# Attention weights applied in plain 4-byte matmuls: what it does to a fused attention and linear kernel

## The chip, the cores and the metric

The kernel runs on one core of a Trainium2 chip. A core has TensorE (PE, matrix products into PSUM, with its weight loads shown apart as PEld), VectorE (DVE), ScalarE (ACT), GpSimd (POOL) and SyncE (SP, which here only issues DMAs). The metric is the device time of the whole program in microseconds (us), as a median of several runs. Each engine runs its own instruction list in order, and the lists meet at semaphores.

## What is computed

A block of a transformer on x of 4 sequences, 1024 tokens and 1024 channels: layer norm, attention with 16 heads of 64 channels, residual; then layer norm, a 1024 x 1024 linear layer, residual. Cut to what matters here:

```python
q, k, v = (split_heads(layernorm(x) @ W + b) for W, b in ((Wq, bq), (Wk, bk), (Wv, bv)))
# local: each block of 128 queries sees 256 keys around it
probs = softmax(einsum('nhbqd,nhbkd->nhbqk', q_blocks, k_windows) / 8)
ctx = einsum('nhbqk,nhbkd->nhbqd', probs, v_windows)
# global: bos, eos and the 62 tokens with the largest |q| of each head see all keys
g_probs = softmax(einsum('nhqd,nhkd->nhqk', q[idx], k) / 8)
g_ctx = einsum('nhqk,nhkd->nhqd', g_probs, v)
ctx = ctx.at[bn, bh, idx].set(g_ctx)
x = x + ctx
x = x + layernorm(x) @ (weight * scale_weight[:, None]).T + bias
```

All of it is wanted at 4-byte precision.

## The kernel before

**Number formats.** TensorE is fed mostly in `F32R`, a 4-byte format that holds fewer mantissa bits. To keep precision, an operand is split in a high part (a copy that rounds to F32R, on ACT or POOL) and a low part (the rest, a subtraction on DVE or POOL), and a product is made from several matmuls of parts. Transposes (`pe.transpose`, a matmul against the identity `ident`) take plain 4-byte `F32` operands, unsplit.

**Stages.** For each of the 4 sequences (`batch`), the transposed, normalised x (`xT_hi`, `xT_lo`) meets the q weights; then a loop runs over 8 pairs of heads. One pass of it is `attend` on PE, ACT and DVE, and `unit` on POOL: 32 units u in all. In a unit, PE works on the attention of one pair of heads, and between its steps projects keys and values of the next pair in eight parts of 12 matmuls (`part(0)` to `part(7)`, `project`, L564, 128x512 each). At the end stands a linear stage (`linear`, L751).

**Local attention of a unit** goes in 4 steps s, each with 2 blocks of queries b for the 2 heads h. `scores` (L662) fills the PSUM tile `score`; DVE takes row maxima (`maxima`), ACT the exponentials with row sums (`exps`, L988) into `probs`; PE transposes these in `turn_p` (L677) into the PSUM tile `turn`. ACT copies `turn` to `pT_hi` (`p_hi_out`, L1001), DVE subtracts to get `pT_lo` (`p_lo_out`, L1380). `weigh` (L687) multiplies by V: for each of the 4 (head, block) groups g, 4 matmuls, `pT_hi` and `pT_lo` as the stationary operand for 2 tiles of keys c, against `v_nat`, which holds the 64 channels of V's high part and the 64 of its low part side by side. So one matmul is 128x128 and g takes 128 columns of the PSUM tile `pv`: sums with V's high part in the first 64, with its low part in the last 64.

**Out of `pv`.** ACT copies the low half (`pv_lo_out`, L1012), DVE adds the high half (`pv_sums`, L1401) into `pv_sum` and frees `pv` for the next step (`pv_free`), and POOL multiplies by the reciprocals of the row sums (`normalise`, L449) into `ctx_out`, one of two buffers by the parity of s. SP stores it to DRAM (`store_ctx`, L255).

**Global attention of a unit** does the same once for all 1024 keys: `turn_gp` (L722), `gp_hi_out`, `gp_lo_out`, then `global_weigh` (L731) with 2 times 9 matmuls of 128x256 (both heads, high and low), `g_lo_out` and `g_out` into `g_ctx`.

**V** comes from `vT` by `turn_v` (L699) into the PSUM tile `misc`, from which `v_hi_out` (ACT) and `v_lo_out` (DVE) make `v_nat`.

**What sets the order** is the program as written: `attend` on each engine is a fixed list, given below. On PE a unit ends with `part(6)`, `part(7)`, `global_weigh`, and the next begins with `scores(0)`.

## Time and profile before

| | us |
|---|---|
| median of 3 runs | 2184.9 (2182.88 to 2185.11) |
| profiled execution | 2185.36 |
| its span | 2183.8 |
| PE busy | 2142.9 (98%) |
| PEld busy | 1825.5 (84%) |
| DVE busy | 1475.5 (68%) |
| ACT busy | 836.9 (38%) |
| POOL busy | 600.7 (28%) |

The span goes from the first to the last instruction of the profiled execution. A busy share says how long an engine had something in hand, not how fast: a matmul's shown duration reaches from its start to a modelled end, and matmuls overlap, so what one costs PE is read from the distance between starts, or from the chain of waits. The granted clock of TensorE is 9 (90% or more of full speed) in every one of 40 slices.

### The profile page before, as it was taken

The page shows a single profiled execution, that of the slowest core. Times are in us where ns is not written, and L with a number is a line of the kernel's source. Part 1 is how long each engine was busy: PE and PEld are TensorE (multiplying, and loading weights), DVE is VectorE, ACT ScalarE, POOL GpSimd, SP SyncE. Part 2 cuts the span into 40 slices and gives each one's busy share as a digit, 9 for nine tenths or more (in the row PEclk, how much of TensorE's full clock was granted, in tenths as well). Part 3 has the DMA queues.
Part 4 walks back from the last instruction along what each step waited for, and adds up shares of the span by engine and source line. Part 5 has one row for each costly group of instructions (what it writes and reads, how often), then busy time and mean ns, then how long its engine had stood idle before and what let it go on. Part 6 is the DMA issues. An engine that isn't in the chain of part 4 may idle for free.

```text
span 2183.8 us, 38335 instructions
## 1 busy us (share of the span) xinstructions
PE 2142.9 (98%) x12768; PEld 1825.5 (84%) x12768; DVE 1475.5 (68%) x2966; ACT 836.9 (38%) x2203; POOL 600.7 (28%) x464
## 2 busy tenths in 40 slices
PE   6999999999999999999999999999999998999999
PEld 5888888888888888888888888888888887888887
DVE  5687667665876776648776767496666675666664
ACT  3334444453344455523444545325445451000000
POOL 2332232224321332243223312433123113121221
PEclk9999999999999999999999999999999999999999
DMA  4332121104322211043122211321113113333331
GB/s 148 96 97 73 60 89 44 53 30 125 99 64 70 74 58 52 30 125 97 63 72 60 71 53 32 99 83 45 53 51 108 34 49 121 132 132 134 127 141 68
DMA packets 116725, 175.38 MB, mean 80 GB/s; under 512 B 16208, under 2 KB 81814, under 8 KB 116624
## 3 DMA queue, kind: packets, MB, share of 16 engines
q1 hardware_dynamic: 108976, 156.30, 22.3%
q10 hardware_dynamic: 4320, 15.73, 1.8%
q0 software_dynamic: 3328, 2.17, 0.5%
q8 instruction: 43, 0.70, 0.1%
q14 instruction: 58, 0.48, 0.1%
HBM read 122.73 MB, written 51.44 MB: 80 GB/s over the span
## 4 chain that ended last, share of the span: by engine, by line
PE 88%; DVE 5%; issue 3%; ACT 2%; POOL 1%; DMA 1%; DVEq 0%; SPq 0%; POOLq 0%; ACTq 0%
PE proj L564 44%; PE proj L751 15%; PE pv L687 9%; PE turn L677 5%; PE score L662 5%; PE pv L731 3%; PE score L712 2%; PE misc L699 1%; PE turn L740 1%; PE turn L722 1%; DVE xT_lo L1276 1%; PE turn L605 1%; ACT probs L988 1%; ACT xT_hi L916 1%; DMA q_store<-in_rows 0%
## 5 line engine op out<-in xcount | busy, mean ns | idle before, releaser
L564 PE MATMUL proj<-xT_hi,w_hi 128*128 128x512 f32 x1568 | 410.0, 403 | 9.7 <-DVE xT_lo L1268 3.8
L564 PE MATMUL proj<-xT_hi,w_lo 128*128 128x512 f32 x1568 | 416.9, 397 | 0.0
L564 PE MATMUL proj<-xT_lo,w_hi 128*128 128x512 f32 x1568 | 389.1, 390 | 0.0
L564 PEld LDWEIGHTS proj<-xT_lo,w_hi 128*128 128x128 f32 x1568 | 294.3, 188 | 63.4
L564 PEld LDWEIGHTS proj<-xT_hi,w_lo 128*128 128x128 f32 x1568 | 287.0, 188 | 63.5
L564 PEld LDWEIGHTS proj<-xT_hi,w_hi 128*128 128x128 f32 x1568 | 281.6, 189 | 66.3 <-issue 5.4
L988 ACT ACTIVATE probs<-score,neg_max 128x256 f32<-128x256 f32 (+1 forms) x512 | 229.2, 460 | 162.3 <-DVE neg_max L1364 98.7
L449 POOL TENSOR_TENSOR ctx_out<-pv_sum,row_inv 128x256 f32<-128x256 f32 x128 | 84.9, 663 | 661.4 <-DVE pv_sum L1401 635.4
L425 POOL CAST w_hi<-w_raw 128x1024 fp32r<-128x1024 f32 x96 | 115.5, 1203 | 515.1 <-PE proj L564 357.8
L427 POOL TENSOR_TENSOR w_lo<-w_raw,w_hi 128x1024 fp32r<-128x1024 f32 x96 | 232.0, 2416 | 7.8
L687 PE MATMUL pv<-v_nat,pT_lo 128*128 128x128 f32 x1024 | 198.1, 275 | 0.0
L687 PE MATMUL pv<-v_nat,pT_hi 128*128 128x128 f32 x1024 | 194.3, 271 | 0.0
L1380 DVE TENSOR_TENSOR pT_lo<-turn,pT_hi 128x512 fp32r<-128x512 f32 x256 | 164.6, 684 | 13.9 <-ACT pT_hi L1001 10.8
L687 PEld LDWEIGHTS pv<-v_nat,pT_hi 128*128 128x128 f32 x1024 | 162.1, 191 | 11.4 <-issue 0.8
L1401 DVE TENSOR_TENSOR pv_sum<-pv,pv_lo 128x256 f32<-128x256 f32 x128 | 54.3, 424 | 153.1 <-ACT pv_lo L1012 138.9
L687 PEld LDWEIGHTS pv<-v_nat,pT_lo 128*128 128x128 f32 x1024 | 155.4, 192 | 0.0
L544 POOL TENSOR_TENSOR q_store<-q_store,bias_b 128x1024 f32<-128x1024 f32 x30 | 71.6, 2389 | 261.2 <-DVE q_store L1631 259.9
L968 ACT ACTIVATE kT_hi<-proj,bk_c 128x512 fp32r<-128x512 f32 x64 | 44.2, 690 | 255.3 <-PE proj L564 159.0
L1001 ACT CAST pT_hi<-turn 128x512 fp32r<-128x512 f32 x256 | 138.7, 594 | 7.6 <-PE turn L677 2.1
L677 PE MATMUL turn<-ident,probs 128*128 128x128 f32 (+1 forms) x1024 | 135.6, 275 | 2.0 <-ACT probs L988 2.0
L1282 DVE TENSOR_TENSOR q_sq<-q_nat 128x512 f32<-128x512 f32 x64 | 69.3, 1083 | 93.9 <-ACT q_nat L938 80.3
L677 PEld LDWEIGHTS turn<-ident,probs 128*128 128x128 f32 (+1 forms) x1024 | 111.8, 137 | 4.2 <-ACT probs L988 3.7
(173 smaller groups left out, 3409.7 us busy)
## 6 DMA issues: line engine op xcount, KB each, us to landing
w_raw<-in_wstream SPq DMA_DIRECT2D x96, 512.0 KB
x_buf<-in_rows SPq DMA_DIRECT2D x55, 512.0 KB, 3.9
q_rows<-q_nat SPq DMA_DIRECT2D x64, 256.0 KB
ctx_rows<-ctx_out SPq DMA_DIRECT2D x128, 128.0 KB, 1.8
q_store<-ctx_rows SPq DMA_DIRECT2D x30, 512.0 KB
out<-q_store ACTq DMA_DIRECT2D x30, 512.0 KB, 2.6
q_store<-in_cols SPq DMA_DIRECT2D x28, 512.0 KB, 4.0
q_store<-in_rows SPq DMA_DIRECT2D x8, 512.0 KB, 5.4
```

What stands on the lines that cost most here:

```text
L425: pool.tensor_copy(w_hi[b][:, :], w_raw[b][:, :]).then_inc(w_hi_set, 1)
L427: pool.tensor_tensor(w_lo[b][:, :], w_raw[b][:, :], w_hi[b][:, :].bitcast(F32), ALU.subtract).then_inc(w_split[b], 1)
L449: pool.tensor_tensor(ctx_out[:, s % 2].rearrange("p b h d -> p h b d"), pv_sum[:, s % 2].rearrange("p (h b) d -> p h b d", h=2), row_inv[: ...
L544: pool.tensor_tensor(lin_hb[:, b, :], lin_h[:, b, :], bias_b[:, :], ALU.add).then_inc(hb_set, 1)
L564: mm = pe.matmul(proj[:, bank, :], w[b][:, k * P:k * P + P], x[:, k, half * HALF:half * HALF + HALF], start=(m == 0), stop=(m == 23), skip ...
L662: mm = pe.matmul(score[:, at:at + hi - lo], qs[r, i * BLK:i * BLK + BLK], ks[r, lo:hi], start=(first and b == 0), stop=stop, skip_group_ch ...
L677: mm = pe.transpose(turn[0:rows, col:col + P], probs[:, src:src + rows], ident[:, :])
L687: mm = pe.matmul(pv[:, g * P:g * P + P], pt[:, (g * 2 + c) * P:(g * 2 + c) * P + P], v_nat[:, 2 * s + b + c, h, :], start=(m == 0), stop=( ...
L751: mm = pe.matmul(proj[:, half, :], x[b][:, k * P:k * P + P], w[:, k, half * 512:half * 512 + 512], start=(m == 0), stop=(m == 23), skip_gr ...
L988: last = act.activation(probs[:, at:at + hi - lo], score[:, at:at + hi - lo], ACT.Exp, bias=neg_max[:, g:g + 1], accum_out=row_sum[:, g:g ...
L1001: act.copy(pT_hi[:, h * 512:h * 512 + 512], turn[:, h * 512:h * 512 + 512]).then_inc(pT_hi_set, 1)
L1380: dve.tensor_tensor(pT_lo[:, cols], turn[:, cols], pT_hi[:, cols].bitcast(F32), ALU.subtract).then_inc(pT_set, 1)
```

## The change

The probabilities are copied out of `turn` once, as plain 4-byte `pT` (ACT, `p_out`, `gp_out`), and V out of `misc` once, as plain 4-byte `v_nat` with 64 columns per head (ACT, `v_nat_out`). `weigh` multiplies them in 8 matmuls of 128x64 per step instead of 16 of 128x128, `global_weigh` in 9 of 128x128 instead of 18 of 128x256. `pv` then holds the full sums, and DVE multiplies them by the reciprocals straight into `ctx_out` (`pv_out`), or into `g_ctx` (`g_out`). POOL's `normalise` is gone, with the subtractions on DVE and the copies of low halves on ACT. The wait for the store of `ctx_out` two steps earlier moves from POOL to DVE.

```diff
-        v_nat = sb("v_nat", [P, TILES + 1, 2, P], F32R)
+        v_nat = sb("v_nat", [P, TILES + 1, 2, HD])
-        pT_hi, pT_lo = sb("pT_hi", [P, SEQ + P], F32R), sb("pT_lo", [P, SEQ + P], F32R)
+        pT = sb("pT", [P, SEQ + P])
...
             def store_ctx(n, hp, s):
-                sp.wait_ge(ctx_set, n * (PAIRS * STEPS) + hp * STEPS + s + 1 + STEPS)
+                sp.wait_ge(pv_free, n * (PAIRS * EVENTS) + hp * EVENTS + s + 2)
...
-                for s in range(STEPS - 1):
-                    normalise(n, hp, s)
                 if value:
                     split_value(n, hp)
-                normalise(n, hp, STEPS - 1)
...
                     for b in range(2):
                         g = h * 2 + b
-                        for m, (pt, c) in enumerate(((pT_hi, 0), (pT_hi, 1), (pT_lo, 0), (pT_lo, 1))):
-                            mm = pe.matmul(pv[:, g * P:g * P + P], pt[:, (g * 2 + c) * P:(g * 2 + c) * P + P],
-                                           v_nat[:, 2 * s + b + c, h, :], start=(m == 0), stop=(m == 3))
+                        for c in range(2):
+                            mm = pe.matmul(pv[:, g * HD:g * HD + HD], pT[:, (g * 2 + c) * P:(g * 2 + c) * P + P],
+                                           v_nat[:, 2 * s + b + c, h, :], start=(c == 0), stop=(c == 1))
...
-                for m, pt in enumerate((pT_hi, pT_lo)):
-                    for j in range(TILES + 1):
-                        col = ((j - 1) % (TILES + 1)) * P
-                        mm = pe.matmul(pv[:, 0:256], pt[:, col:col + P], v_nat[:, j, :, :].rearrange("p h d -> p (h d)"),
-                                       start=(m == 0 and j == 0), stop=(m == 1 and j == TILES))
+                for j in range(TILES + 1):
+                    col = ((j - 1) % (TILES + 1)) * P
+                    mm = pe.matmul(pv[:, 0:P], pT[:, col:col + P], v_nat[:, j, :, :].rearrange("p h d -> p (h d)"),
+                                   start=(j == 0), stop=(j == TILES))
...
-            def p_hi_out(u, s):
+            def p_out(u, s):
                 for h in range(2):
                     act.wait_ge(p_turned, 2 * (u * EVENTS + s) + h + 1)
-                    act.copy(pT_hi[:, h * 512:h * 512 + 512], turn[:, h * 512:h * 512 + 512]).then_inc(pT_hi_set, 1)
+                    act.copy(pT[:, h * 512:h * 512 + 512], turn[:, h * 512:h * 512 + 512]).then_inc(pT_set, 1)
...
-            def pv_sums(u, s):
-                dve.wait_ge(pv_lo_set, u * EVENTS + s + 1)
-                dve.wait_ge(ctx_set, u * STEPS + s + STEPS - 1)
-                dve.tensor_tensor(pv_sum[:, s % 2], pv4[:, :, 0:HD], pv_lo[:, :, :], ALU.add).then_inc(pv_free, 1)
+            def pv_out(u, s):
+                dve.wait_ge(pv_done, u * EVENTS + s + 1)
+                dve.wait_ge(inv_set, u * EVENTS + s + 1)
+                dve.wait_ge(ctx_stored[s % 2], u * (16 * STEPS // 2) + 16 * (s // 2) + 16)
+                dve.tensor_tensor(ctx_out[:, s % 2].rearrange("p b h d -> p h b d"),
+                                  pv[:, 0:4 * HD].rearrange("p (h b d) -> p h b d", h=2, b=2),
+                                  row_inv[:, 4 * s:4 * s + 4].rearrange("p (h b) -> p h b", h=2).unsqueeze(3)
+                                  .broadcast_to([P, 2, 2, HD]), ALU.mult).then_inc(pv_free, 1)
...
-                dve.wait_ge(pv_lo_set, u * EVENTS + EVENTS)
-                dve.tensor_tensor(g_sum[0:64, :], pv4[0:64, 0, 0:HD], pv_lo[0:64, 0, :], ALU.add)
-                dve.tensor_tensor(g_sum[64:P, :], pv4[64:P, 1, 0:HD], pv_lo[64:P, 0, :], ALU.add).then_inc(pv_free, 1)
-                dve.wait_ge(pv_free, u * EVENTS + EVENTS + 1)
-                dve.tensor_scalar(g_ctx[:, bass.ds(hp, 1), :].rearrange("p a d -> p (a d)"), g_sum[:, :],
-                                  row_inv[:, 4 * STEPS:4 * STEPS + 1], None, ALU.mult).then_inc(g_set, 1)
+                dve.wait_ge(pv_done, u * EVENTS + EVENTS)
+                dve.wait_ge(inv_set, u * EVENTS + EVENTS)
+                for h in range(2):
+                    r = slice(h * HD, h * HD + HD)
+                    last = dve.tensor_scalar(g_ctx[r, bass.ds(hp, 1), :].rearrange("p a d -> p (a d)"),
+                                             pv[r, h * HD:h * HD + HD], row_inv[r, 4 * STEPS:4 * STEPS + 1], None, ALU.mult)
+                last.then_inc(pv_free, 1)
```

On PE, in a unit, the weighing of step 1 stands between the projection's matmuls and the transposes of step 2. Before:

```order
L564 MATMUL proj<-xT_hi,w_hi 128x512 x8
L564 MATMUL proj<-xT_hi,w_lo 128x512 x4
L681 REGISTER_ALU
L687 MATMUL pv<-v_nat,pT_hi 128x128 x2
L687 MATMUL pv<-v_nat,pT_lo 128x128 x2
L687 MATMUL pv<-v_nat,pT_hi 128x128 x2
L687 MATMUL pv<-v_nat,pT_lo 128x128 x2
L687 MATMUL pv<-v_nat,pT_hi 128x128 x2
L687 MATMUL pv<-v_nat,pT_lo 128x128 x2
L687 MATMUL pv<-v_nat,pT_hi 128x128 x2
L687 MATMUL pv<-v_nat,pT_lo 128x128 x2
L668 ISA
```

And the same place now (line numbers are those of the changed program):

```order
L544 MATMUL proj<-xT_hi,w_hi 128x512 x8
L544 MATMUL proj<-xT_hi,w_lo 128x512 x4
L661 REGISTER_ALU
L667 MATMUL pv<-v_nat,pT 128x64 x8
L648 ISA
L657 MATMUL turn<-ident,probs 128x128 x4
```

Sixteen matmuls are eight of half the width; their place has not moved.

On DVE, the stretch of a unit from the maxima of step 1 to those of step 2 (`neg_max` are the maxima, `row_inv` the reciprocals of the row sums, `top_idx` belongs to the search for the global tokens). Before:

```order
L1364 TENSOR_REDUCE neg_max<-score 128x2 x2
L1390 REGISTER_ALU
L1394 RECIPROCAL row_inv<-row_sum 128x4
L1317 MAX_INDEX top_idx<-top_val,x_norm 8x8
L1305 REGISTER_ALU
L1346 REGISTER_ALU
L1349 TENSOR_TENSOR v_nat<-misc,v_nat 128x2x64
L1401 TENSOR_TENSOR pv_sum<-pv,pv_lo 128x256
L1379 REGISTER_ALU
L1380 TENSOR_TENSOR pT_lo<-turn,pT_hi 128x512
L1379 REGISTER_ALU
L1380 TENSOR_TENSOR pT_lo<-turn,pT_hi 128x512
```

And now:

```order
L1318 TENSOR_REDUCE neg_max<-score 128x2 x2
L1331 REGISTER_ALU
L1333 RECIPROCAL row_inv<-row_sum 128x4
L1280 MAX_INDEX top_idx<-top_val,x_norm 8x8
L1268 REGISTER_ALU
L1338 ISA
L1339 TENSOR_TENSOR ctx_out<-pv,row_inv 128x2x2x64
L1313 REGISTER_ALU
L1318 TENSOR_REDUCE neg_max<-score 128x2 x2
```

The three subtractions for V and the probabilities are gone, the addition has become the multiplication that POOL did, and the maxima of the next step stand right behind it.

## Rows read from the trace of the kernel before

**Rows 1.** the page: busy us of each engine (share of span), granted clock

```profile
PE 2142.9 (98%) x12768; PEld 1825.5 (84%) x12768; DVE 1475.5 (68%) x2966; ACT 836.9 (38%) x2203; POOL 600.7 (28%) x464
...
PEclk9999999999999999999999999999999999999999
```

**Rows 2.** waits of PE, whole span: total us, times, longest

```profile
PE score L599 <- DVE q_store L1223: 15.2, 1, 15.2
PE proj L751 <- DVE qT_lo L1471: 4.3, 1, 4.3
...
PE turn L677 <- ACT probs L988: 2.0, 9, 0.3
PE turn L740 <- issue: 1.9, 1, 1.9
PE pv L731 <- DVE pT_lo L1386: 1.5, 1, 1.5
```

**Rows 3.** chain of waits, 826 to 846 us: start, us, what

```profile
833.08 1.74 PE pv L687 x16
...
838.62 5.46 PE proj L564 x24
```

**Rows 4.** timeline of PE, end of a unit: start us, us, group

```profile
837.59 1.04 PE L722 MATMUL turn<-ident,probs 128*128 128x128 f32 x8
838.38 2.07 PE L564 MATMUL proj<-xT_hi,w_hi 128*128 128x512 f32 x8
...
842.10 1.98 PE L564 MATMUL proj<-xT_lo,w_hi 128*128 128x512 f32 x8
843.92 1.24 PE L731 MATMUL pv<-v_nat,pT_hi 128*128 128x256 f32 x9
844.99 1.24 PE L731 MATMUL pv<-v_nat,pT_lo 128*128 128x256 f32 x9
846.16 0.50 PE L662 MATMUL score<-kT_hi,qT_hi 64*128 64x192 f32 x4
```

**Rows 5.** weight loads by shape: busy us, mean ns of one

```profile
L687 PEld LDWEIGHTS pv<-v_nat,pT_lo 128*128 128x128 f32 x1024 | 155.4, 192 | 0.0
...
L722 PEld LDWEIGHTS turn<-ident,probs 128*128 128x128 f32 x224 | 25.4, 140 | 3.8
...
L615 PEld LDWEIGHTS score<-ident,norms 128*8 128x8 f32 x64 | 5.5, 87 | 1.9
...
L722 PEld LDWEIGHTS turn<-ident,probs 128*64 128x64 f32 x32 | 3.6, 111 | 0.0
```

**Rows 6.** groups of PE by shape, same columns

```profile
L564 PE MATMUL proj<-xT_lo,w_hi 128*128 128x512 f32 x1568 | 389.1, 390 | 0.0
...
L731 PE MATMUL pv<-v_nat,pT_lo 128*128 128x256 f32 x288 | 39.7, 283 | 0.0
```

**Rows 7.** groups of DVE by shape, same columns

```profile
L1380 DVE TENSOR_TENSOR pT_lo<-turn,pT_hi 128x512 fp32r<-128x512 f32 x256 | 164.6, 684 | 13.9 <-ACT pT_hi L1001 10.8 <-issue 0.2
...
L1401 DVE TENSOR_TENSOR pv_sum<-pv,pv_lo 128x256 f32<-128x256 f32 x128 | 54.3, 424 | 153.1 <-ACT pv_lo L1012 138.9 <-issue 13.6
```

**Rows 8.** the group on POOL that goes, from the page

```profile
L449 POOL TENSOR_TENSOR ctx_out<-pv_sum,row_inv 128x256 f32<-128x256 f32 x128 | 84.9, 663 | 661.4 <-DVE pv_sum L1401 635.4
```

**Rows 9.** the copy on ACT that goes, by shape

```profile
L1012 ACT COPY pv_lo<-pv 128x256 f32<-128x256 f32 x128 | 47.6, 372 | 109.7 <-PE pv L687 109.7
```

**Rows 10.** timeline of ACT, one local step: the four Exp of step 1 end

```profile
812.94 0.48 ACT L988 ACTIVATE probs<-score,neg_max 128x256 f32<-128x256 f32 x1
813.29 0.21 ACT L988 ACTIVATION_READ_ACCUMULATOR probs<-score,neg_max 128x1 f32 x1
```

**Rows 11.** timeline of PE behind them: the transposes that need those Exp

```profile
814.83 1.06 PE L677 MATMUL turn<-ident,probs 128*128 128x128 f32 x8
```

**Rows 12.** the tile ctx_rows: its stores, and DMA time to landing

```profile
L255 SPq DMA_DIRECT2D ctx_rows<-ctx_out x128: 372/373/539, 166.0 to 1809.8; - x128
...
DMA to landing us min/median/max: 1.8/1.8/9.4
```

More of the change, by code:

```diff
@@ L969, in k_hi_out, with v_nat_out @@
                                bias=bk_c[:, bass.ds(hp, 1)]).then_inc(k_hi_set[h], 1)
-            def v_hi_out(u, g):
+            def v_nat_out(u, g):
                 act.wait_ge(m_turned, u * MISC + g + 1)
                 for rows, j, step, count, col in V_PIECES[g]:
-                    last = act.copy(v_nat[0:rows, j:j + step * (count - 1) + 1:step, :, 0:HD],
+                    last = act.copy(v_nat[0:rows, j:j + step * (count - 1) + 1:step, :, :],
                                     misc[0:rows, col:col + count * P].rearrange("p (t h d) -> p t h d", h=2, d=HD))
-                last.then_inc(m_hi_set, 1)
+                last.then_inc(m_set, 1)
             def gq_hi_out(u):
@@ L1046, in attend @@
                     ahead_hi(0)
-                v_hi_out(u, 0)
+                v_nat_out(u, 0)
                 exps(u, 0)
@@ L1051, in attend @@
                     ahead_hi(1)
-                v_hi_out(u, 1)
-                p_hi_out(u, 0)
+                v_nat_out(u, 1)
+                p_out(u, 0)
                 exps(u, 1)
@@ L1056, in attend @@
                 columns(1)
-                v_hi_out(u, 2)
-                pv_lo_out(u, 0)
-                p_hi_out(u, 1)
+                v_nat_out(u, 2)
+                p_out(u, 1)
                 exps(u, 2)
                 columns(2)
-                pv_lo_out(u, 1)
-                p_hi_out(u, 2)
+                p_out(u, 2)
                 exps(u, 3)
@@ L1066, in attend @@
                     out(1, 0)
-                pv_lo_out(u, 2)
                 gq_hi_out(u)
-                p_hi_out(u, 3)
+                p_out(u, 3)
                 columns(4)
@@ L1343, in top_rows @@
                     dve.wait_ge(base_set, n + 2)
-            def v_lo_out(u, g):
-                dve.wait_ge(m_hi_set, u * MISC + g + 1)
-                for rows, j, step, count, col in V_PIECES[g]:
-                    tiles = slice(j, j + step * (count - 1) + 1, step)
-                    last = dve.tensor_tensor(v_nat[0:rows, tiles, :, HD:P],
-                                             misc[0:rows, col:col + count * P].rearrange("p (t h d) -> p t h d", h=2, d=HD),
-                                             v_nat[0:rows, tiles, :, 0:HD].bitcast(F32), ALU.subtract)
-                last.then_inc(m_set, 1)
             def gq_lo_out(u):
-                dve.wait_ge(m_hi_set, u * MISC + MISC)
+                dve.wait_ge(m_hi_set, u + 1)
                 dve.tensor_tensor(gq_lo[:, :], misc[:, 0:P], gq_hi[:, :].bitcast(F32), ALU.subtract).then_inc(m_set, 1)
@@ L1374, in global_maxima @@
                                   negate=True).then_inc(max_set, 2)
-            def p_lo_out(u, s):
-                for h in range(2):
-                    cols = slice(h * 512, h * 512 + 512)
-                    dve.wait_ge(pT_hi_set, 2 * (u * EVENTS + s) + h + 1)
-                    dve.tensor_tensor(pT_lo[:, cols], turn[:, cols], pT_hi[:, cols].bitcast(F32),
-                                      ALU.subtract).then_inc(pT_set, 1)
-            def gp_lo_out(u):
-                dve.wait_ge(pT_hi_set, 2 * (u * EVENTS + EVENTS))
-                dve.tensor_tensor(pT_lo[:, 0:1024], turn[:, :], pT_hi[:, 0:1024].bitcast(F32), ALU.subtract)
-                dve.tensor_tensor(pT_lo[:, 1024:1152], misc[:, 0:P], pT_hi[:, 1024:1152].bitcast(F32),
-                                  ALU.subtract).then_inc(pT_set, 2)
             def inverses(u, s):
                 dve.wait_ge(exp_set, 2 * (u * EVENTS + s + 1))
-                if s < STEPS:
-                    dve.wait_ge(ctx_set, u * STEPS + s + 1)
                 size = 4 if s < STEPS else 1
                 dve.reciprocal(row_inv[:, 4 * s:4 * s + size], row_sum[:, 4 * s:4 * s + size]).then_inc(inv_set, 1)
-            pv4 = pv[:, :].rearrange("p (g d) -> p g d", g=4)
-            def pv_sums(u, s):
-                dve.wait_ge(pv_lo_set, u * EVENTS + s + 1)
-                dve.wait_ge(ctx_set, u * STEPS + s + STEPS - 1)
-                dve.tensor_tensor(pv_sum[:, s % 2], pv4[:, :, 0:HD], pv_lo[:, :, :], ALU.add).then_inc(pv_free, 1)
+            def pv_out(u, s):
[6 more added lines that the diff above has]
+                                  .broadcast_to([P, 2, 2, HD]), ALU.mult).then_inc(pv_free, 1)
             def pad_q(n, u, hp, half):
@@ L1505, in attend @@
                 columns(1)
-                v_lo_out(u, 2)
-                pv_sums(u, 0)
-                p_lo_out(u, 1)
+                pv_out(u, 0)
                 maxima(u, 2)
@@ L1512, in attend @@
                 columns(2)
-                pv_sums(u, 1)
-                p_lo_out(u, 2)
+                pv_out(u, 1)
                 if ahead:
@@ L1525, in attend @@
                     lin_moments(0, 0, 0)
-                pv_sums(u, 2)
+                pv_out(u, 2)
                 gq_lo_out(u)
-                p_lo_out(u, 3)
                 if ahead:
@@ L1540, in attend @@
                     k_lo_out(n, hp + 1, 0)
-                pv_sums(u, 3)
+                pv_out(u, 3)
                 if not last:
```

47 lines of the change are left out of this document (9 added, 38 removed).

## The prediction

> **What bounds the kernel now.** I read the page first, then PE's waits, then one steady unit in the chain and the timeline. PE is busy 2142.9 of 2183.8 us at the full clock [rows 1]; 15.2 us of the rest is the start, and the four other waits that this change could touch are 9.7 us together [rows 2]. In the steady unit the chain never leaves PE: weighing follows projection follows weighing [rows 3]. DVE, ACT and POOL wait for PE, not the reverse. So a microsecond taken from them is worth nothing, and one added to PE's own list is paid 32 or 128 times. The whole question is what PE pays for a weighing.
>
> **What a weighing costs now.** The 16 matmuls of a local step hold the chain for 1.74 us, 0.109 us each [rows 3]. The 18 of the global one take 846.16 - 843.92 = 2.24 us, 0.124 each [rows 4]. Over 32 units: 128 x 1.74 = 223 us and 32 x 2.24 = 72 us.
>
> **What such a pair of weight load and matmul is made of.** A matmul of 512 columns shows 390 ns, one of 256 columns 283 [rows 6]: 107/256 = 0.42 ns a column, the 2.4 GHz level, so 27, 53 and 107 ns for 64, 128 and 256 columns. A weight load of a plain 4-byte operand shows 87, 111 and 140 ns for 8, 64 and 128 columns: 84 ns that don't hold up the next, and 56 ns of loading for 128 columns. A load of an F32R part shows 192, so 108 ns of loading [rows 5]. Now compare with what a pair costs from start to start:
> - F32R, 128 columns: load 108, stream 53, and 109 measured [rows 3]. That is the longer of the two: the load runs under the stream of the matmul before. For 256 columns 108 and 107, measured 124; for 512, 108 and 214, measured (843.92 - 842.10)/8 = 227 [rows 4]. The same.
> - Plain 4-byte (the transposes): load 56, stream 53, and (838.38 - 837.59)/8 = 99 measured [rows 4]. That is near the sum, 109, and far from the longer, 56. Here the load doesn't seem to run under the stream.
>
> **The change on PE.** A local step becomes 8 matmuls of 64 columns, the global one 9 of 128, all with plain 4-byte operands. The trace of before has plain operands only in transposes, which move values and don't multiply them at full precision, so a true product isn't shown and must be bounded. The products kept so far are four (high and low by high and low), and the new matmul must make the same four. I take it as two passes, one for each part of the stationary operand, each with a load of its own and with both parts of the moving operand streamed: 2 x 64 = 128 columns in a local pass, 2 x 128 = 256 in a global one. That is exactly the work of the present matmuls, in pairs: 16 passes a step, 18 for the global one. What differs is whether the loads hide.
>
> I take the load at 108 ns (a load of a part, as the present ones are) and, as in the only rows with plain operands, in line with the stream:
> - local: (108 + 53) x 16 = 2.58 us against 1.74, +0.84, x 128 = +107 us;
> - global: (108 + 107) x 18 = 3.87 us against 2.24, +1.63, x 32 = +52 us.
>
> Bounds of this term. Below: one load and one short stream per matmul, at the price of one transpose pair, 0.099: 0.79 and 0.89 us, so -122 and -43 = -165 us. Above: four passes, each with a load of 108 in line with its 64 or 128 columns: 4 x 135 x 8 = 4.32 us and 4 x 161 x 9 = 5.80 us, +330 and +114 = +444 us. Both ends are far; I stay with the two serial passes because they stand on measured pieces. Four passes with the cheaper load of 56 come to the same by another way: 4 x 83 x 8 = 2.66 and 4 x 109 x 9 = 3.92 us, +118 and +54 = +172.
>
> The rule that bears on the number of passes speaks against the change. The Trainium skill (FP8 and Floating Point Precision, TensorE Precision Notes) has a true 4-byte product go through the array four times, high by high, high by low, low by high, low by low; it doesn't say how often weights are loaded, and no row here shows it. The sum by it is anything from the fastest rival below to the slowest.
>
> **The change on the other engines, all of it beside PE's work.**
> - DVE loses the subtractions for probabilities, 256 x 684 ns = 165 us busy and more for the global ones and V; the addition of 424 ns becomes a multiplication of the same shape from the same PSUM tile, at about the same price [rows 7]. ACT loses 128 copies of 372 ns [rows 9], POOL 128 multiplications, 85 us [rows 8]. All are at 68, 38 and 28% busy [rows 1] and were waiting: value nothing, save for the waits of PE that they end. Those are 1.5 us for `pT_lo` before the global weighing, and parts of the 1.9 and 4.3 us at the start of the linear stage [rows 2]. I take -3 us; at most it is their sum and the 2.0 on `probs`, -10, and at least 0.
> - `pT` is ready on ACT's copy, without the subtraction behind it, and `pv` is free after one DVE instruction instead of ACT and DVE. Both come earlier than they are needed already.
> - DVE takes over the wait for the store of `ctx_out` two steps before. Behind it in DVE's list stand the maxima of the next step, for which ACT's Exp and then PE's transposes wait. A store lands in 1.8 us, 9.4 at worst [rows 12], and between two steps lie, twice, a weighing of 1.74 us [rows 3] and 12 projection matmuls of 0.227 [rows 4], 8.9 us without the rest; I take 0. If it failed once in a unit by 1 us, it would be 32 us.
> - SP's stores now wait for DVE rather than POOL, one instruction earlier. Nothing.
>
> **Sum.** Against the profiled execution: 2185.4 + 107 + 52 - 3 = 2341 us. The median of the runs is 0.5 us lower, which changes nothing.
>
> **The rivals.**
> 1. *The loads hide after all (not slower).* Plain passes then cost what F32R ones of equal columns do: 16 x 0.109 = 1.74 and 18 x 0.124 = 2.24 us, a difference of 0, and 2182 with the waits. For it: the work per pass is the same, and the present loads hide. Against it: the transposes' 99 ns. Its place is every weighing, and what decides is whether a load in the midst of two passes may run under the stream; if a local pass stays under 110 ns, the change is not slower.
> 2. *Serial, but with the transposes' load of 56.* Local 16 x 109 = 1.74 us, no change; global 18 x 163 = 2.93, +0.69 x 32 = +22: 2204.
> 3. *One load, four streams (faster).* A local matmul is then an F32R one of 256 columns, 0.124: 0.99 us, -0.75 x 128 = -96; a global one is one of 512, 0.227: 2.05 us, -0.19 x 32 = -6: 2080 with the waits. Against it: a part is loaded for each product that has another stationary part, and there are two. PE would then come earlier to the transposes behind: the Exp of that step end at 813.50 and PE wants them at 814.83 [rows 10, 11], so 0.75 us can be taken from the step before ACT is waited for.
> 4. *Four whole pairs per matmul.* At the transposes' 99 ns, whatever the columns: 4 x 99 x 8 = 3.17 us, +1.43 x 128 = +183, and 4 x 99 x 9 = 3.56, +1.32 x 32 = +42: 2407. At 109 ns a pair, 3.49 and 3.92 us: +224 and +54, 2460. For it: the transposes are the plain matmuls that the trace has, and they needn't form products of parts. The Trainium skill (TensorE: Matmul & The Clock Gate, Terms) calls transpose mode four times faster for 4-byte operands, which by itself would put an ordinary plain matmul at four such pairs and the time at this rival's 2407; nothing in the trace shows it.
>
> **How the numbers follow.** Forecast (serial passes, 2341, or 2353 by the cheap-load variant) 0.42; rival 1 0.24; rival 2 0.08; rival 3 0.13; rival 4 0.13. About 0.2% (4.4 us) is what can be told from no change. Slower by more: forecast, rivals 2 and 4 and a hundredth of rival 1, 0.64. Faster by more: rival 3 and a third of rival 1, in which the ended waits bring more than 3 us, 0.21. The rest, 0.15, is the same. The likeliest case by itself spans 2310 to 2370. The range goes from 2172, which takes in rival 1 with all waits gained, to 2430, which takes in the nearer form of rival 4; outside stay rival 3 and the dearer rival 4, 0.18.
>
> **What would show it.** In the profile after, the chain's piece for 8 local matmuls at 2.6 us and for the 9 global ones at 3.9, with PE still at 98% and no new waits, each unit longer by 4 x 0.84 + 1.63 = 5.0 us; loads of `pT` at about 192 ns, twice as many in the records as there are matmuls in the program. Pieces of 1.74 and 2.24 us would mean rival 1, about 1 us rival 3, over 3 us rival 4. Wrong in another way would be waits of PE on `probs` or `pv`, or DVE waiting at `ctx_out` for a DMA. A total near 2341 with other pieces would be luck, not the theory.

## The result, and the profile after

| | before | after |
|---|---|---|
| median of 4 runs each on one chip, us | 2184.5 (2182.9 to 2185.1) | 2165.3 (2164.1 to 2165.5) |
| ratio, 95% interval | | 0.991 (0.990 to 0.993) |
| span of the profiled execution, us | 2183.8 | 2163.8 |
| VectorE, ScalarE, GpSimd busy | 68, 38, 28% | 56, 36, 24% |

The change takes 19.3 us off, 0.9%. The forecast was 2341; the range ended at 2172, above the result. PE's granted clock is at the full level (2.4 GHz) in both kernels, but for a stretch near the start and one at the start of the linear stage; the second is not equally long in the two profiles, and is taken up below.

The page: PE's busy time falls by 11.9 us from that of [rows 1], its share and its number of recorded matmuls don't move.

```profile
PE 2131.0 (98%) x12768; PEld 1819.7 (84%) x12768; DVE 1206.7 (56%) x2486; ACT 783.3 (36%) x2011; POOL 509.1 (24%) x336
```

The local weighing, as one line's instructions: duration min/median/max, first and last start.

```profile
L667 PEld LDWEIGHTS pv<-v_nat,pT x2048: 187/192/245, 160.3 to 1786.8; 128*128 128x128 f32 x187
L667 PE MATMUL pv<-v_nat,pT x2048: 217/275/275, 160.4 to 1786.9; 128*128 128x64 f32 x187
```

The program has 128 steps of 8 such matmuls, 1024; the records hold 2048, each with a weight load of 192 ns like those of [rows 5]. So a plain 4-byte product is two passes with a load each.

The chain of waits in a steady unit (start, us, what), to be read against [rows 3]: 16 passes still hold it for 1.73 us.

```profile
820.75 1.73 PE pv L667 x16
```

The timeline of PE at the same unit's end, against [rows 4]: the global weighing goes from 838.45 to 840.55, 2.10 us, where it was 2.24.

```profile
838.45 2.17 PE L710 MATMUL pv<-v_nat,pT 128*128 128x128 f32 x18
840.55 0.50 PE L642 MATMUL score<-kT_hi,qT_hi 64*128 64x192 f32 x4
```

PE's waits, against [rows 2]: the one for `pT_lo` is gone, that for `probs` has fallen from 2.0 to 0.3 us, and `qT_lo` is as long as before.

```profile
PE proj L730 <- DVE qT_lo L1413: 4.3, 1, 4.3
...
PE turn L719 <- DVE x_norm L1186: 1.4, 1, 1.4
...
PE turn L657 <- ACT probs L967: 0.3, 1, 0.3
```

These waits explain some 4 us, the global weighing 32 x 0.14 = 4.5. To find the rest I measured every unit on PE's timeline, from the end of one global weighing to the end of the next (the end is taken as the start of the matmul behind it). The fourth sequence has no next one to prepare, so its last units stand apart:

| us | ordinary unit | 7th unit, sequences 1 to 3 | 8th unit, sequences 1 to 3 | last two, sequence 4 | from the last unit to PE's last matmul |
|---|---|---|---|---|---|
| before | 42.45 | 42.67 | 45.28 | 44.16, 48.63 | 362.15 |
| after | 42.26 | 42.26 | 42.17 | 42.17, 46.59 | 360.79 |

20 ordinary units give 3.8 us, three 7th ones 1.2, three 8th ones 9.3, the last two of sequence 4 give 2.0 each and the end 1.4; with 0.2 at the start, 19.9 of the 20.0 us between the spans. Nearly half of the gain lies in three units of 32, which the steady unit of the prediction doesn't show.

The 1.4 us at the end are the clock's, not the change's, but for a tenth. At the start of the linear stage the granted clock lies at the lower level (1.2 GHz) for 6.8 us in the profile of before and for 3.4 us in that of after (the line of before, then that of after; window, us, PE busy, granted clock, DMA share, GB/s):

```profile
1834.60:1841.40 6.80, 5.29 (x13) 0.50 0.40 150
...
1817.50:1820.90 3.40, 3.40 (x10) 0.50 0.40 116
```

Experiment 3 below is the kernel after with matmuls added only behind this stage. Its profile has 6.8 us at the lower level here, and 362.06 us from the last unit to the last projection where after has 360.79. So this term changes from one execution to the next under one and the same program.

Here is the 8th unit of the first sequence before, on PE (start, us, group, idle before and its releaser):

```profile
449.67 0.50 PE L662 MATMUL score<-kT_hi,qT_hi 64*128 64x192 f32 x4
...
452.38 2.08 PE L564 MATMUL proj<-xT_hi,w_hi 128*128 128x512 f32 x8 [1.20 <-DVE xT_lo L1276]
...
455.58 0.63 PE L699 MATMUL misc<-ident,vT 128*128 128x128 f32 x4 [0.19 <-DVE v_nat L1349]
...
469.69 0.66 PE L677 MATMUL turn<-ident,probs 128*128 128x128 f32 x4 [0.19 <-ACT probs L988]
470.60 0.66 PE L677 MATMUL turn<-ident,probs 128*128 128x128 f32 x4 [0.26 <-ACT probs L988]
```

And the same unit after:

```profile
448.14 0.50 PE L642 MATMUL score<-kT_hi,qT_hi 64*128 64x192 f32 x4
...
449.41 2.07 PE L544 MATMUL proj<-xT_hi,w_hi 128*128 128x512 f32 x8
...
465.72 1.04 PE L657 MATMUL turn<-ident,probs 128*128 128x128 f32 x8
```

From the unit's start the projection begins 452.38 - 449.67 = 2.71 us in before, 1.27 after: 1.44 us. The transposes at 469.69 begin 20.02 in, those at 465.72 after 17.58: by then it is 2.44, and the unit ends 3.11 apart. The four waits marked here sum to 1.84 us, less than is lost: a wait counts only while the engine has nothing in hand, and the stretches that merely thin out carry none. Compare starts, not only waits.

What DVE does ahead of that projection, before:

```profile
441.60 4.33 DVE L1276 TENSOR_TENSOR xT_lo<-q_store,xT_hi 128x512 fp32r<-128x512 f32 x2
445.86 1.21 DVE L1385 TENSOR_TENSOR pT_lo<-turn,pT_hi 128x1024 fp32r<-128x1024 f32 x1
...
447.85 4.29 DVE L1276 TENSOR_TENSOR xT_lo<-q_store,xT_hi 128x512 fp32r<-128x512 f32 x2
```

And POOL beside it, splitting the next projection weights:

```profile
441.09 1.50 POOL L425 CAST w_hi<-w_raw 128x1024 fp32r<-128x1024 f32 x1 [8.16 <-PE proj L564]
442.67 2.72 POOL L427 TENSOR_TENSOR w_lo<-w_raw,w_hi 128x1024 fp32r<-128x1024 f32 x1
...
447.53 1.30 POOL L425 CAST w_hi<-w_raw 128x1024 fp32r<-128x1024 f32 x1 [1.11 <-issue]
448.91 2.69 POOL L427 TENSOR_TENSOR w_lo<-w_raw,w_hi 128x1024 fp32r<-128x1024 f32 x1
```

Each pair of subtractions for the next sequence's columns, which have both inputs in SBUF, takes 4.3 us. Taken one by one, the first of a pair takes 1.5 us beside POOL's cast and the second 2.9 beside POOL's subtraction; the second of the first pair reads so:

```profile
443.06 2.88 DVE L1276 TENSOR_TENSOR xT_lo<-q_store,xT_hi 128x512 fp32r<-128x512 f32 x1
```

After, both subtractions of the first pair begin before POOL's cast does, at 439.92, and both stay at 0.68 to 0.69 us. One collision is left, spread over the next two subtractions, 1.46 and 2.88 us:

```profile
439.31 1.29 DVE L1239 TENSOR_TENSOR xT_lo<-q_store,xT_hi 128x512 fp32r<-128x512 f32 x2
...
440.58 1.46 DVE L1239 TENSOR_TENSOR xT_lo<-x_buf,xT_hi 128x512 fp32r<-128x512 f32 x1
441.96 3.48 DVE L1239 TENSOR_TENSOR xT_lo<-q_store,xT_hi 128x512 fp32r<-128x512 f32 x2
```

Alone a pair takes 1.29 us; beside POOL up to 4.33. This is what the experiments had to test, beside the price of the passes.

### The profile page after: what moved, and what is told of

Its sections match the earlier page's. It is cut to its first block, busy times and chain, and to the rows that moved or that the text cites. A ratio compares the mean times of both kernels' runs of the same rounds, so it can differ in the third digit from the quotient of the medians.

```text
span 2163.8 us, 36898 instructions
## 1 busy us (share of the span) xinstructions
PE 2131.0 (98%) x12768; PEld 1819.7 (84%) x12768; DVE 1206.7 (56%) x2486; ACT 783.3 (36%) x2011; POOL 509.1 (24%) x336
## 4 chain that ended last, share of the span: by engine, by line
PE 94%; DVE 3%; issue 1%; POOL 1%; DMA 1%; ACT 0%; SPq 0%; DVEq 0%; POOLq 0%; ACTq 0%
PE proj L544 48%; PE proj L730 15%; PE pv L667 10%; PE score L642 5%; PE turn L657 5%; PE pv L710 3%; PE score L692 2%; PE misc L679 2%; PE turn L702 1%; PE turn L719 1%; PE turn L585 1%; DMA q_store<-in_rows 1%; DVE top_idx L1280 0%; DVE x_norm L1282 0%; DVE top_val L1278 0%
## 5 line engine op out<-in xcount | busy, mean ns | idle before, releaser
L420 POOL CAST w_hi<-w_raw 128x1024 fp32r<-128x1024 f32 x96 | 106.1, 1105 | 1184.0 <-PE proj L544 912.9
L667 PEld LDWEIGHTS pv<-v_nat,pT 128*128 128x128 f32 x2048 | 246.0, 192 | 10.8
L667 PE MATMUL pv<-v_nat,pT 128*128 128x64 f32 x2048 | 242.2, 271 | 0.0
L980 ACT COPY pT<-turn 128x512 f32<-128x512 f32 x256 | 137.9, 593 | 119.4 <-PE turn L657 119.4
L1318 DVE TENSOR_REDUCE neg_max<-score 128x2 f32<-128x512 f32 x128 | 82.5, 686 | 145.9 <-PE score L642 145.9
L1339 DVE TENSOR_TENSOR ctx_out<-pv,row_inv 128x256 f32<-128x256 f32 x128 | 54.1, 423 | 165.4 <-PE pv L667 142.1
L1263 DVE SCALAR_TENSOR_TENSOR kT_lo<-proj,bk_c,kT_hi 128x512 fp32r<-128x512 f32 x64 | 47.8, 747 | 147.3 <-ACT kT_hi L947 147.2
L1321 DVE TENSOR_REDUCE neg_max<-score 128x1 f32<-128x192 f32 (+1 forms) x256 | 82.2, 384 | 49.1 <-PE score L642 49.1
L967 ACT ACTIVATION_READ_ACCUMULATOR probs<-score,neg_max 128x1 f32 x512 | 104.3, 204 | 0.0
```

Source lines behind the costliest of these rows:

```text
L420: pool.tensor_copy(w_hi[b][:, :], w_raw[b][:, :]).then_inc(w_hi_set, 1)
L667: mm = pe.matmul(pv[:, g * HD:g * HD + HD], pT[:, (g * 2 + c) * P:(g * 2 + c) * P + P], v_nat[:, 2 * s + b + c, h, :], start=(c == 0), sto ...
L967: last = act.activation(probs[:, at:at + hi - lo], score[:, at:at + hi - lo], ACT.Exp, bias=neg_max[:, g:g + 1], accum_out=row_sum[:, g:g ...
L980: act.copy(pT[:, h * 512:h * 512 + 512], turn[:, h * 512:h * 512 + 512]).then_inc(pT_set, 1)
L1318: last = dve.tensor_reduce(neg_max[:, g:g + 2], score4[:, 2 * h:2 * h + 2, a:z], AX.X, ALU.max, negate=True)
L1321: last = dve.tensor_reduce(neg_max[:, g + b:g + b + 1], score4[:, 2 * h + b, a:z], AX.X, ALU.max, negate=True)
```

## The experiments

All ratios are against the kernel before, run on the same chip.

**1. Only PE's matmuls changed.** The kernel before with plain products in its two weighings; DVE, ACT and POOL keep all their instructions.

```diff
-                        for m, (pt, c) in enumerate(((pT_hi, 0), (pT_hi, 1), (pT_lo, 0), (pT_lo, 1))):
-                            mm = pe.matmul(pv[:, g * P:g * P + P], pt[:, ...],
+                        for c in range(2):
+                            mm = pe.matmul(pv[:, g * P:g * P + HD], pT_hi[:, ...],
...
-                act.copy(pv_lo[:, :, :], pv4[:, :, HD:P]).then_inc(pv_lo_set, 1)
+                act.mul(pv_lo[:, :, :], pv4[:, :, 0:HD], 0.0).then_inc(pv_lo_set, 1)
```

> The kernel before with only TensorE's weighing changed: 8 plain 4-byte matmuls of 64 columns a step, 9 of 128 in the global one. ACT, DVE and POOL keep every instruction (the subtractions give zeros, and the low half of pv is the high one times zero). Theory (the plain matmul is two passes at the F32R price, and most of the 19 us came from DVE's relief in the last unit of each sequence): only the 0.19 us a unit from the global weighing, 32 x 0.19 = 6 us, so 2178 us, and the last unit of a sequence still takes 45.3 us. Rival (the gain is all in the matmuls): 2165 us.

Measured: 2179.9 against 2185.0, ratio 0.998 (0.997 to 0.999), -5.0 us. A steady unit falls from 42.45 to 42.26, exactly as after; the 8th stays at 45.24. Its chain:

```profile
822.37 1.73 PE pv L687 x16
```

So the plain products alone cost nothing and bring a quarter of the gain, nearly all of it in the global weighing.

**2. Only the relief.** The kernel after, with the F32R matmuls back and the low parts as constant zeros, so that DVE, ACT and POOL have the changed work and PE the old.

```diff
-                        for c in range(2):
-                            mm = pe.matmul(pv[:, g * HD:g * HD + HD], pT[:, ...],
+                        for m, (pt, c) in enumerate(((pT, 0), (pT, 1), (pZ, 0), (pZ, 1))):
+                            mm = pe.matmul(pv[:, g * P:g * P + P], pt[:, ...],
```

> The changed kernel with TensorE's F32R matmuls of before put back (16 of 128 columns a step, 18 of 256): ACT, DVE and POOL do what the changed kernel has them do. The low parts are left out: they are tiles of zeros, so the context is computed from high parts alone. Theory: the waits of PE in the last unit of each sequence go as in the changed kernel (about 13 us), the 6 us in the matmuls don't: 2171 us, last units of 42.4 us. Rival (all in the matmuls): 2184 us.

Measured: 2171.5, ratio 0.994 (0.992 to 0.996), -13.5 us. Steady units 42.45, 8th ones 42.37. The parts nearly add up: 5.0 + 13.5 = 18.5 of 19.3. Some 70% of the gain is work taken from engines that PE was said not to wait for.

**3. The price of each kind of matmul.** The kernel after, with 12 blocks of 48 matmuls or transposes behind the last projection.

```diff
+            block(48, lambda i: pe.transpose(turn[:, 0:P], probs[:, ...], ident[:, :]))
+            block(48, lambda i: pe.transpose(turn[0:64, 0:P], probs[:, ...], ident[:, :]))
+            block(48, lambda i: pe.matmul(sc[:, 0:64], pT[:, ...], vT[:, 0:64], ...))
...
+            block(48, lambda i: pe.matmul(sc[:, 0:16], xT_hi[:, ...], xT_lo[:, 0, 0:16], ...))
```

> The changed kernel with twelve blocks of 48 matmuls on TensorE behind its last matmul, whose results nobody reads: the price of each kind by itself. Theory (each plain product is two passes of load and stream, loads of 108 ns under the streams): 0.22 us a matmul with 16, 32 or 64 moving columns, 0.23 with 128, 0.45 with 256; F32R 0.109 with 16 or 128. With 64 stationary columns half the load: 0.11 to 0.13 for 64 moving ones. Rival (the load stands in line, as I predicted): 0.32 us for 64 moving columns, 0.24 for 16, 0.43 for 128. The transposes at 0.099: if their load stands in line, 64 stationary columns bring them to about 0.07; if something in the stream of 128 columns sets them, they stay at 0.099.

One run, 2281.6 us with the blocks. The timeline of PE over the blocks (in a group, 64*... or 128*... is the stationary operand's rows and columns, then the output):

```profile
2160.26 5.41 PE L875 MATMUL turn<-ident,probs 128*128 128x128 f32 x48
2165.50 5.40 PE L876 MATMUL turn<-ident,probs 128*64 128x128 f32 x48
2170.74 10.83 PE L877 MATMUL score<-vT,pT 128*128 128x64 f32 x96
2181.41 18.06 PE L878 MATMUL score<-vT,pT 128*128 128x16 f32 x96
...
2212.66 20.89 PE L880 MATMUL score<-vT,pT 128*128 128x256 f32 x96
2233.47 5.81 PE L881 MATMUL score<-vT,pT 128*64 128x64 f32 x96
2239.12 7.79 PE L882 MATMUL score<-vT,pT 128*64 128x16 f32 x96
2246.84 10.50 PE L883 MATMUL score<-xT_lo,xT_hi 128*128 128x128 f32 x48
2257.15 10.35 PE L884 MATMUL score<-xT_lo,xT_hi 128*128 128x16 f32 x48
2267.35 5.36 PE L885 MATMUL score<-xT_lo,xT_hi 128*64 128x128 f32 x48
```

And the stretches of it (window, us, PE busy, granted clock, DMA share, GB/s):

```profile
2160.30:2165.40 5.10, 5.10 (x49) 1.00 0.25 103
2165.60:2170.60 5.00, 5.00 (x48) 1.00 0.01 3
2170.80:2181.40 10.60, 10.60 (x97) 1.00 0.00 0
2181.50:2199.30 17.80, 17.80 (x97) 0.58 0.00 1
2199.30:2212.60 13.30, 13.30 (x97) 0.80 0.01 1
2212.70:2233.40 20.70, 20.70 (x98) 1.00 0.00 1
...
2239.20:2246.80 7.60, 7.60 (x98) 0.70 0.01 2
2246.90:2257.10 10.20, 10.20 (x49) 0.50 0.00 0
2257.20:2267.30 10.10, 10.10 (x49) 0.50 0.01 2
```

From start to start, a plain pass of 64 columns costs (2181.41 - 2170.74)/96 = 0.111 us, one of 256 columns 0.217, and one of 64 columns with half the stationary operand 0.059. So with 128 stationary columns the load sets the price up to where the stream is longer, and never is it the sum, 0.161 and 0.323. The blocks with a clock between the levels, plain passes of 16 and of 128 moving columns, give no price. (A plain pass streams each column twice: 2 x 64 x 0.42 = 54 ns, and 2 x 256 x 0.42 = 215, as measured.) F32R passes at the 1.2 GHz level cost 0.215 with 128 moving columns and 0.213 with 16, and 0.108 with half the stationary operand: load-bound as well. The Trainium skill (TensorE: Matmul & The Clock Gate, LDWEIGHTS (loading the stationary operand)) gives a load in ns as its column count divided by 1.2, which makes an estimate of 107 ns for 128 columns. The passes of 128 stationary columns at the full level agree, 0.108 us in the chain and 0.111 here; those at the 1.2 GHz level take twice that.

The first two rows break the inference behind the forecast. The transposes cost 0.109 us with 128 stationary columns and 0.109 with 64, both at the full level. A load in line with the stream would have made the second cheaper by half a load, 28 ns. What does hold a transpose at 0.109 is left open: fewer moving columns were not tried.

**4. The normalisation back on POOL.** The kernel after, in which DVE copies `pv` out, POOL multiplies and sets off the store.

```diff
-                dve.tensor_tensor(ctx_out[:, s % 2]..., pv[:, 0:4 * HD]..., row_inv[...], ALU.mult).then_inc(pv_free, 1)
+                dve.tensor_copy(pv_sum[:, s % 2]..., pv[:, 0:4 * HD]).then_inc(pv_free, 1)
...
+                pool.tensor_tensor(ctx_out[:, s % 2]..., pv_sum[:, s % 2]..., row_inv[...], ALU.mult).then_inc(ctx_set, 1)
```

> The changed kernel with the normalisation back on POOL: DVE copies pv to SBUF (same size as its multiplication), POOL multiplies by the reciprocals, as before. Theory (moving the normalisation is worth nothing, since DVE's list is as long and POOL is idle most of the time): 2165 us. Rival (part of the gain came from taking POOL's 85 us and its handshake with DVE away): 2170 us or more, with waits of DVE on ctx_out.

Measured: 2164.7, 0.991 (0.989 to 0.993): the same as after. Moving the multiplication is worth nothing here.

**5 to 7. Which property of the subtractions counts?** All on the kernel after. Number 5 puts subtractions of the old shapes back on DVE, on constants, for nobody; number 6 puts a one-column DVE instruction into the chain from ACT to PE instead, so that PE waits for DVE again but DVE is as light as after; number 7 has number 5's load in the last two units of each sequence only.

```diff
+                waste_v(hp, 0)
...
+                waste_v(hp, 1)
+                waste_p(hp, 0)
...
+                dve.wait_ge(pT_hi_set, 2 * (u * EVENTS + s) + h + 1)
+                dve.tensor_copy(junk[:, 3 + 2 * s + h:4 + 2 * s + h], ident[:, 0:1]).then_inc(pT_set, 1)
...
+                if isinstance(hp, int) and hp >= PAIRS - 2:
```

> The changed kernel with subtractions of the sizes removed put back into DVE's list at their old places, on constants in SBUF; nobody waits for them and they wait for nobody. Theory A (the waits in the last units come from DVE's list being too long there): most of the 13.5 us of relief is lost, 2176 to 2179 us. Theory B (they come from the subtraction standing in the chain from ACT's copy to the next matmul): 2165 us.

> The changed kernel with DVE put back into the chain only: after each of ACT's copies of V and of the probabilities, DVE waits for it, does an instruction of one column, and only that lets PE go on. Theory A (length of DVE's list): 2165 to 2168 us. Theory B (the chain): 2176 us or more.

> As the run with all the unwaited subtractions, but only in the last two of the eight units of a sequence. Theory A (only those units are short of DVE, for they also carry the low parts of the next sequence's x): the same time as with all of them. Rival (the other six units lose a little each too): nearer to 2165 us by a quarter of the difference or more.

Measured: 2168.9 (0.992, 0.991 to 0.994), 2164.7 (0.991, 0.989 to 0.992) and 2167.5 (0.992, 0.990 to 0.994). The extra link costs nothing, so it isn't latency. The dummy load costs 2.7 us against the runs of before on its own chip, 3.6 against after, far less than the 11 us or more of theory A, and not where I looked for it: the 8th units stay at 42.17, and it is the 7th unit of sequence 4 that grows from 42.17 to 46.69 (43.70 in number 7). The load alone doesn't give the 3.1 us per 8th unit.

Nor is that one unit the price of the real subtractions. The dummies read two SBUF operands, the real ones read one of theirs from PSUM, and at 1712.32 us two dummies take 4.54 us beside POOL's additions of the bias. PE then waits 0.85 and 0.26 us for `probs`, in number 7 as in number 5. Behind these waits the granted clock of number 5 falls:

```profile
1725.60:1729.20 3.60, 3.60 (x10) 0.50 0.00 0
```

In number 7 it stays at 1.00 over the same stretch. The 3.0 us between the two numbers here are the clock's.

**8. A stream twice as wide.** The kernel after, with 128 moving columns in the local product, of which half the result is thrown away; DVE reads the other half in two instructions.

```diff
-                            mm = pe.matmul(pv[:, g * HD:g * HD + HD], pT[:, ...], v_nat[:, 2 * s + b + c, h, :],
+                            mm = pe.matmul(pv[:, g * P:g * P + P], pT[:, ...], v_nat[:, 2 * s + b + c, :, :]...,
```

> The changed kernel with twice the moving columns in each local product: both heads' V (128 columns) though only 64 of the results are read; the output is complete, and DVE reads them in two instructions instead of one. Theory (the stream runs over the next load of 108 ns and is paid only above it): a pass goes from 0.108 to 0.117 us, as in the global weighing, 128 x 16 x 0.009 = +18 us, 2183. Rival (load and stream in line, as I predicted): 53 ns more a pass, +109 us, 2274.

Measured: 2170.2, 0.993 (0.992 to 0.995), 4.9 us over after, or 4.0 if each is taken against the runs of before on its own chip: over 2048 passes, 2.0 to 2.4 ns each. In line, 54 ns more stream in each of them would be 109 us. The chain:

```profile
821.81 1.78 PE pv L667 x16
```

0.111 us a pass instead of 0.108. The stream of 107 ns still lies under the load of 108. My expectation of 0.117 a pass and 2183 us, taken from the global weighing, was too high: those 18 passes are 0.117 on average up to the start of the next group, but 0.112 from one to the next inside the group.

**9 to 11. What makes the 8th unit late.** All on the kernel after: number 9 has the real subtractions, which PE waits for; number 10 lets DVE's dummy subtractions wait for ACT while PE doesn't wait for them; number 11 has the old way out of `pv` (ACT copies, DVE adds, POOL multiplies) and no subtractions.

```diff
+                    dve.tensor_tensor(pT_lo[:, cols], turn[:, cols], pT[:, cols], ALU.subtract).then_inc(pT_set, 1)
...
+                    dve.wait_ge(pT_set, 2 * (u * EVENTS + s) + h + 1)
+                    waste(P, 512, s % 2 * 1024 + h * 512)
...
+                act.mul(pv_lo[:, :, :]..., pv[:, 0:4 * HD], 0.0).then_inc(pv_lo_set, 1)
```

> The changed kernel with DVE's subtractions back as they were, reading PSUM behind ACT's copies and with PE waiting for them; the way out of pv stays the new one. Theory C (neither length nor link alone, but the two together: DVE is held by ACT, then works 1.4 us or more, and the low parts of the next x slip into POOL's weight splits): most of the 13.5 us relief is lost, 2174 to 2178 us, last units of 45 us. Rival (it was the way out of pv, with its four engines): 2165 us.

> As the run with unwaited subtractions of constants, but each waits for ACT's copy as the real ones did; PE waits for none of them. If what matters is DVE held back in its own list (waiting for ACT, then working): near the run with the real subtractions, 2174 us or more. If PE's own wait for them matters: 2169 us, as without the waits.

> The changed kernel with the old way out of pv (ACT copies, here times zero; DVE adds; POOL multiplies), and no subtractions. Theory C: 2165 to 2168 us, last units of 42.2 us. Rival (the way out of pv): 2174 us or more.

Measured: 2166.6 (0.992, 0.990 to 0.993), 2169.3 (0.993, 0.991 to 0.995) and 2166.5 (0.992, 0.990 to 0.994). The 8th units: 42.39, 42.40 and 42.20. Number 9 was expected at 2174 us or more and misses by over 7. Neither half of the old work makes them late; both together, which is number 1, give 45.24. The reason stands in DVE's rows at this place. With the real subtractions (number 9) both pairs of column subtractions miss POOL's split:

```profile
438.87 1.29 DVE L1240 TENSOR_TENSOR xT_lo<-q_store,xT_hi 128x512 fp32r<-128x512 f32 x2
...
444.03 1.28 DVE L1240 TENSOR_TENSOR xT_lo<-q_store,xT_hi 128x512 fp32r<-128x512 f32 x2
```

With the old way out (number 11) the first is caught, the second not:

```profile
439.31 4.33 DVE L1271 TENSOR_TENSOR xT_lo<-q_store,xT_hi 128x512 fp32r<-128x512 f32 x2
...
444.58 1.28 DVE L1271 TENSOR_TENSOR xT_lo<-q_store,xT_hi 128x512 fp32r<-128x512 f32 x2
```

Before, both are, and in number 1 too. One collision of 3.0 us fits into DVE's slack ahead of the next projection, two don't. In sequence 4 the last two units go to 43.01 and 47.68 in number 9, and stay at 42.16 and 46.57 in number 11: there, the subtractions cost time without the old way out.

**12. The collision removed.** The kernel before, in which POOL splits only the first column of each key and value weight inside the units (the projections use stale weights; POOL's instructions and signals stay).

```diff
-                pool.tensor_copy(w_hi[b][:, :], w_raw[b][:, :]).then_inc(w_hi_set, 1)
+                pool.tensor_copy(w_hi[b][:, 0:w], w_raw[b][:, 0:w]).then_inc(w_hi_set, 1)
...
+                split(n, i, 0, n * BUFS + PAIRS // 2 + 2 + hp, 0, n * SLICES + i, w=1)
```

> The kernel before with POOL's splits of the key and value weights inside the units cut to one column: the weights used there are stale, so keys and values are not the right ones. Theory D (in the last units DVE's SBUF to SBUF subtractions for xT_lo take 2.1 us instead of 0.65 while POOL splits weights, and this is what makes DVE late): the last units of a sequence fall from 45.3 to 43 us or less, and the time to 2176 us or less. Rival (DVE's list is too long with or without it): 45 us and 2183 us or more.

Measured: 2176.4 against 2184.3, 0.996 (0.995 to 0.998), -7.9 us, with everything that the change removes still in place. The 8th units fall from 45.28 to 42.80, 3 x 2.5 = 7.4 us, and the 7th ones from 42.67 to 42.45, 0.7 in all; sequence 4 (44.16, 48.73) doesn't move. DVE's two pairs, at the place of those 4.33 and 4.29 us:

```profile
439.59 1.28 DVE L1276 TENSOR_TENSOR xT_lo<-q_store,xT_hi 128x512 fp32r<-128x512 f32 x2
...
443.14 1.29 DVE L1276 TENSOR_TENSOR xT_lo<-q_store,xT_hi 128x512 fp32r<-128x512 f32 x2
```

That is the collision shown: the same instructions of DVE, in the same order, lose 3 us a pair only while POOL reads and writes whole weights. POOL's list is shorter here too, which could have helped by itself if DVE had waited for POOL. It didn't: in before, DVE has no idle time at this place from 439.40 to 455.43 us. The Trainium skill (SBUF — State Buffer, SBUF: two separate sides) has the rule: a DVE operation with two SBUF inputs and a GpSimd operation that reads SBUF take one pair of ports, exclusively and for a whole instruction, and the later one blocks. The rows agree: each subtraction of the pair ends 0.54 to 0.55 us behind the POOL instruction that it met (443.13 against 442.59, 445.94 against 445.39), little less than the 0.68 it takes alone.

Sequence 4 has a collision of its own, which this experiment leaves in place. In its 7th unit before, two `xT_lo` subtractions, at 1759.74 and 1762.55, take 2.9 us each beside POOL's additions of the bias, `pT_lo` is made behind them, and PE waits 1.54 us for it. In after nothing of POOL's stands at that place. What the last two units gain, 2.0 us each, is in part this collision and in part the subtractions themselves (0.8 and 1.1 in number 9, where nothing collides there); no run separates the two.

No kernel beat the one after by more than the runs differ.

## Why the prediction was wrong

Two steps failed. The first, the load in line, put the forecast 159 us too high. With it mended the sum comes to some 2177 us, and what is left, the 12 us down to 2165 and past the end of the range at 2172, is in the main the second: the relief of the other engines.

- **PE bounds the kernel, and only its own list counts.** True of a steady unit, and false of the whole. The chain and timeline of [rows 3, 4] are one ordinary unit; in the 8th unit of a sequence DVE also makes the next sequence's columns, and PE waits for it. "Worth nothing" was read from one stretch and applied to 32.
- **Two passes, each with its own load, each streaming both parts.** Right: twice as many records, loads of 192 ns as foreseen, and in experiment 3 a price of 0.217 for 256 moving columns, which is two streams of each.
- **The load in line with the stream.** This is the first step that failed, and by far the larger: 2.58 and 3.87 us were predicted for a local and a global weighing, 1.73 and 2.10 measured, so +107 and +52 us became about -1 and -4.5. The inference was that the transposes' 99 ns (109 in the block of 48) is the sum of 56 and 53. Experiment 3 shows it isn't: half the load leaves it at 109. Two numbers that happen to sum to a third had been taken for a mechanism, against the F32R rows that showed the opposite for the same engine. Experiment 8 shows the hiding from the other side.
- **Rival 1** had it: a local pass under 110 ns, and no slower. It was given 0.24. Its time, 2182, missed what the other engines give, and the 4.5 us of the global weighing: a global pass is a little cheaper than an F32R one of the same stream, 2.10/18 = 0.117 against 0.124, which neither had.
- **The relief of the other engines, -3 us.** The second step that failed, mis-sized: 13.5 (experiment 2). The waits named there did end, `pT_lo` 1.5 us, `probs` 1.7, `x_norm` 0.5 of 1.9, and `qT_lo` lost nothing; but the 9.3 us of the 8th units, of which experiment 12 gives 7.4 to the collision, were not in the sum. The list of waits holds 3.6 us for them, in three waits of up to 1.2 (this row was not among the four waits that the prediction added up), where comparing unit lengths shows two and a half times that.
- **The wait for the store moved to DVE at no cost.** Right: experiment 4, where POOL has this wait again, takes the same time. DVE's idle time ahead of the multiplication is put down to PE, 23.0 us of it to nothing and none to a DMA, and the multiplication costs what the addition of [rows 7] did:

```profile
L1339 DVE TENSOR_TENSOR ctx_out<-pv,row_inv 128x256 f32<-128x256 f32 x128 | 54.1, 423 | 165.4 <-PE pv L667 142.1 <-issue 23.0
```

- **Rivals 2 to 4** fall with the pieces: a global pass isn't dearer, a local step isn't 0.99 us, nor over 3. At the same 128 moving columns a plain product costs 2 x 0.111 us (experiment 8), two transposes and not the four of rival 4.
- **Two readings were off and changed nothing.** 256 x 684 ns is 175 us; the 165 are the row's busy time. And the 9.4 us at worst of [rows 12] is not a store's: that view takes in the reads of `ctx_rows`, and 9.4 is the landing of `qT_cur`. How late the latest store lands is not shown.

## What to carry to other kernels

In a row of matmuls, price each as the longer of its weight load and its stream before you price it as their sum, and doubt a sum that rests on one kind of instruction; a block of the same operation with half the load settles it. Before you call an engine's relief worthless, measure the length of every unit of the loop, not the waits of a typical one: a few units carry extra work, and there the "idle" engine is the bound. Read the granted clock of each stretch that you compare, in both kernels: here it gave 1.4 us of the gain and 3.0 of an experiment's loss. A dummy instruction stands for a real one only if its operands lie in the same memories. Where VectorE reads two SBUF operands while GpSimd works on SBUF, shifting either by a microsecond or two can matter more than what either computes.

## What the runs showed of the hardware that I had not expected

- A plain 4-byte product of 128 stationary and 64 moving columns costs 0.22 us, two load-bound passes, and a product of twice the moving columns almost the same (0.111 us a pass in experiment 8). A plain transpose of 128 columns costs 0.109, with a whole or half a stationary operand.
- The granted clock fell while PE had no idle time. In experiment 3 it is 1.00 in the block of 64 columns and 0.58 on average in the block of 16 that follows, where PE is busy for 17.80 of 17.80 us. In the block of 128 columns it is 0.80 on average and in those of 256 and of 64 with half the stationary operand 1.00; in the next block of 16 it is 0.70, and in the F32R blocks behind it 0.50, the 1.2 GHz level. There a load-bound pass cost twice as much, 0.215 us: the load goes with the clock.
- A DVE subtraction of 512 columns from two SBUF operands takes 0.68 us alone, 1.5 beside POOL's cast and 2.9 beside POOL's subtraction of 1024 columns. In turn POOL's cast takes 1.04 us alone and 1.57 when DVE's subtraction began 0.01 us before it.
- The collision's cost isn't additive: experiments 9 and 11 have each half of the removed work and lose 0.2 and 0.0 us in an 8th unit, experiment 1 has both and loses 3.1.
